# Down pass of a two-layer block on one Trainium2 core: every second weight tile's high half on VectorE, y's rows on SyncE's queue, weight sums ahead of the decode steps

## What is computed

```python
w = NF4_CODE[q.reshape(-1)]                       # 16 codes, q is int32
w = w.reshape(-1, BLOCK) * absmax[:, None]        # one scale for 64 values
g = jnp.einsum('bsh,mh->bsm', x, Wg)              # 2048 tokens, 1024 -> 3584
u = jnp.einsum('bsh,mh->bsm', x, Wu)
h = jax.nn.silu(g) * u
return jnp.einsum('bsm,hm->bsh', h, Wd)           # 3584 -> 1024
x = x + ffn(layernorm(x))                         # the last line of the block
```

## Time and profile before

| | us |
|---|---|
| median of 3 runs | 2045.4 (2044.11 to 2045.6) |
| the profiled execution's own time | 2050.94 |
| its span | 2049.1 |
| TensorE busy | 1948.0 (95%) |
| VectorE busy | 1632.8 (80%) |
| ScalarE busy | 1542.9 (75%) |
| TensorE's granted clock, mean | 0.982 of full speed |

### The profile page before, as it was taken

The page is one execution under the profiler, slowest core; times in us unless marked ns, Lnnn a source line. Parts: engine busy times, 40 slices in busy tenths (PEclk is TensorE's granted clock), DMA queues, the critical chain, the costliest instruction groups (busy, mean ns, idle before and its releaser), DMA issues.

```text
span 2049.1 us, 29927 instructions
## 1 busy us (share of the span) xinstructions
PE 1948.0 (95%) x9872; PEld 987.3 (48%) x9872; DVE 1632.8 (80%) x2716; ACT 1542.9 (75%) x2856; POOL 450.4 (22%) x688
## 2 busy tenths in 40 slices
PE   8989999989999999999999999999999895889999
PEld 3468778744444444444444444444444342334444
DVE  6757789876988898898889889888877677975764
ACT  3768778747989988988998998897999798921100
POOL 0012544540111111121111112112222232222221
PEclk9999999999999999999999999999999997999999
DMA  9012679573644655555564645556677796755443
GB/s 338 25 42 78 186 223 219 168 280 78 154 124 116 138 136 128 124 142 127 120 150 116 136 124 135 128 124 146 166 199 192 192 227 184 177 172 175 165 147 141
DMA packets 387850, 314.63 MB, mean 154 GB/s; under 512 B 327280, under 2 KB 327280, under 8 KB 385776
## 3 DMA queue, kind: packets, MB, share of 16 engines
q1 hardware_dynamic: 334544, 136.00, 30.9%
q0 software_dynamic: 51072, 176.72, 26.3%
q10 hardware_dynamic: 2080, 0.01, 0.1%
HBM read 154.31 MB, written 82.31 MB: 115 GB/s over the span
## 4 chain that ended last, share of the span: by engine, by line
PE 36%; ACT 24%; DVE 21%; issue 10%; DMA 2%; POOL 0%; DVEq 0%; ACTq 0%; SPq 0%; POOLq 0%
PE ps L1978 17%; PE ps L1936 15%; ACT sq L240 8%; ACT sq L236 6%; DVE w L249 4%; DVE tail L2103 2%; ACT halves L287 2%; ACT tail L2009 2%; DVE halves L294 2%; PE ps L1341 1%; ACT tail L2024 1%; PE ps L1302 1%; DMA T<-halves 1%; DVE tail L2069 1%; PE ps L1377 1%
## 5 line engine op out<-in xcount | busy, mean ns | idle before, releaser
L1936 PE MATMUL ps<-T,wS 128*128 128x512 f16 x4704 | 1020.0, 379 | 10.5 <-ACT ps L1993 6.3
L1936 PEld LDWEIGHTS ps<-T,wS 128*128 128x128 f16 x4704 | 458.6, 98 | 568.4 <-issue 15.0
L240 ACT ACTIVATE sq<-sq 128x512 f32<-128x512 f32 x1008 | 572.2, 623 | 0.0
L249 DVE SCALAR_TENSOR_TENSOR w<-sq,w 128x512 f32<-128x512 f32 x672 | 468.5, 697 | 121.2 <-ACT sq L240 108.2
L236 ACT ACTIVATE sq<-q 128x512 f32<-128x512 int32 x672 | 409.4, 628 | 79.8 <-DVE w L249 78.7
L1978 PE MATMUL ps<-T,tail 128*128 128x512 f16 x1584 | 353.3, 385 | 38.9 <-DVE T L2130 34.1
L1978 PEld LDWEIGHTS ps<-T,tail 128*128 128x128 f16 x1584 | 156.4, 99 | 233.4 <-DVE T L2130 36.0
L287 ACT CAST halves<-w 128x512 f16<-128x512 f32 x252 | 154.7, 614 | 52.1 <-DVE w L249 41.0
L1978 PE MATMUL ps<-T,wS 128*128 128x512 f16 x768 | 174.1, 388 | 12.7 <-DVE tail L2150 9.1
L1860 POOL DMA_DIRECT2D keep_h<-tail x196 | 106.3, 542 | 339.6 <-DVE tail L2103 335.1
L2034 ACT CAST T<-w 128x512 f16<-128x512 f32 x56 | 34.5, 617 | 192.6 <-DVE w L2124 192.5
(11 more groups left out here) (216 smaller groups left out, 1861.3 us busy)
## 6 DMA issues: line engine op xcount, KB each, us to landing
keep_h<-tail POOLq DMA_DIRECT2D x196, 256.0 KB, 2.9
tail<-keep_h POOLq DMA_DIRECT2D x66, 512.0 KB, 4.4
wS<-keep_h POOLq DMA_DIRECT2D x32, 512.0 KB, 4.2
q<-in_L_ffn_down_q POOLq DMA_DIRECT2D x56, 256.0 KB, 3.9
q<-in_L_ffn_up_q POOLq DMA_DIRECT2D x52, 256.0 KB, 2.9
q<-in_L_ffn_gate_q POOLq DMA_DIRECT2D x48, 256.0 KB, 3.2
keep_x<-T SPq DMA_DIRECT2D x38, 256.0 KB, 2.8
T<-in_x SPq DMA_DIRECT2D x9, 1024.0 KB, 5.4
```

The source lines that it names most:

```text
L240: nc.scalar.activation(place, place, ACT.Square, bias=b, scale=a).then_inc(un.s_act, 1)
L249: nc.vector.scalar_tensor_tensor(out=un.w[:, buf, :], in0=un.sq[:, (i - 1) % SQ_RING, :], scalar=FACTORS[i - 1][1], in1=un.w[:, buf, :], o ...
L1936: last = nc.tensor.matmul(ps[:, bank, :], un.wS[:, z % SLOTS, a, kt, :], t.Tp[side][product][:, :, b, kt, :], start=fresh and n == 0, stop ...
```

## The change

It has four parts. Every second piece of the down matrix (odd numbers) gets its high half from a VectorE copy between factors 1 and 2 of the next unit, with a semaphore of its own. The quota of VectorE in groups 0 to 2 is 6 instructions in every step. The loads and stores of y's rows go from GpSimd's queue to SyncE's, between the transposes: the stores of a group at the start of the next, the loads at its third step. In VectorE's list of a step the sums stand ahead of the decode instructions; ScalarE's list keeps its order.

```diff
--- before.py
+++ after.py
@@ -130,6 +130,16 @@
     return 2 * pair + (quad in (1, 2)), 2, quad // 2, v % 4
 
 
+def high_on_dve(z):
+
+    return z >= GATE_UP_PIECES and (z - GATE_UP_PIECES) % 2 == 1
+
+
+def highs_on(dve, z):
+
+    return sum(high_on_dve(n) == dve for n in range(z + 1))
+
+
 def last_piece_in(buf, before):
 
     for z in range(before - 1, -1, -1):
@@ -178,6 +188,7 @@
         self.s_add = sem("s_add")
         self.s_turned = [sem(f"s_turned{i}") for i in range(HALF_RING)]
         self.s_whi = sem("s_whi")
+        self.s_dhi = sem("s_dhi")
         self.s_wlo = sem("s_wlo")
 
 
@@ -287,10 +298,21 @@
     nc.scalar.copy(un.halves[:, z % HALF_RING, 0, :], un.w[:, buf, :]).then_inc(un.s_whi, 1)
 
 
+def piece_hi_dve(nc, dve, un, z):
+
+    v = z - GATE_UP_PIECES
+    dve.wait_ge(un.s_fac, STEPS * (GATE_UP_UNITS + v + 1))
+    dve.wait_ge(un.s_turned[z % HALF_RING], 16 * (z // HALF_RING))
+    nc.vector.tensor_copy(un.halves[:, z % HALF_RING, 0, :], un.w[:, v % 4, :]).then_inc(un.s_dhi, 1)
+
+
 def piece_lo(nc, dve, un, z):
 
     buf = PIECE_BUF[z % PIECES] if z < GATE_UP_PIECES else (z - GATE_UP_PIECES) % 4
-    dve.wait_ge(un.s_whi, z + 1)
+    if high_on_dve(z):
+        dve.wait_ge(un.s_dhi, highs_on(True, z))
+    else:
+        dve.wait_ge(un.s_whi, highs_on(False, z))
     nc.vector.scalar_tensor_tensor(out=un.halves[:, z % HALF_RING, 1, :], in0=un.w[:, buf, :], scalar=1.0,
                                    in1=un.halves[:, z % HALF_RING, 0, :], op0=ALU.mult, op1=ALU.subtract).then_inc(un.s_wlo, 1)
 
@@ -327,8 +349,12 @@
     for v in range(DOWN_UNITS):
         for i in range(STEPS):
             yield factor(nc, dve, un, t, GATE_UP_UNITS + v, i)
+            if i == 1 and v > 0 and high_on_dve(GATE_UP_PIECES + v - 1):
+                yield piece_hi_dve(nc, dve, un, GATE_UP_PIECES + v - 1)
             if i == 2 and v > 0:
                 yield piece_lo(nc, dve, un, GATE_UP_PIECES + v - 1)
+    if high_on_dve(GATE_UP_PIECES + DOWN_UNITS - 1):
+        yield piece_hi_dve(nc, dve, un, GATE_UP_PIECES + DOWN_UNITS - 1)
     yield piece_lo(nc, dve, un, GATE_UP_PIECES + DOWN_UNITS - 1)
 
 
@@ -355,9 +381,10 @@
     for v in range(DOWN_UNITS):
         for i in range(OPS):
             yield square(nc, act, un, GATE_UP_UNITS + v, i)
-            if i == 4 and v > 0:
+            if i == 4 and v > 0 and not high_on_dve(GATE_UP_PIECES + v - 1):
                 yield piece_hi(nc, act, un, GATE_UP_PIECES + v - 1)
-    yield piece_hi(nc, act, un, GATE_UP_PIECES + DOWN_UNITS - 1)
+    if not high_on_dve(GATE_UP_PIECES + DOWN_UNITS - 1):
+        yield piece_hi(nc, act, un, GATE_UP_PIECES + DOWN_UNITS - 1)
 
 
 class Plan:
@@ -367,11 +394,13 @@
         fac, add, lo, sq, hi = {}, {}, {}, {}, {}
         d = a = 0
 
-        def dve_unit(u, late):
+        def dve_unit(u, late, copied=None):
             nonlocal d
             for i in range(STEPS):
                 d += 1
                 fac[u, i] = d
+                if i == 1 and copied is not None and high_on_dve(copied):
+                    d += 1
                 for z in late.get(i, ()):
                     d += 1
                     lo[z] = d
@@ -405,17 +434,22 @@
             lo[z], hi[z] = d, a
         for v in range(DOWN_UNITS):
             z = GATE_UP_PIECES + v - 1
-            dve_unit(GATE_UP_UNITS + v, {2: (z,)} if v else {})
-            act_unit(GATE_UP_UNITS + v, {4: (z,)} if v else {})
-        d, a, z = d + 1, a + 1, GATE_UP_PIECES + DOWN_UNITS - 1
-        lo[z], hi[z] = d, a
+            dve_unit(GATE_UP_UNITS + v, {2: (z,)} if v else {}, z if v else None)
+            act_unit(GATE_UP_UNITS + v, {4: (z,)} if v and not high_on_dve(z) else {})
+        z = GATE_UP_PIECES + DOWN_UNITS - 1
+        d += 2 if high_on_dve(z) else 1
+        lo[z] = d
+        if not high_on_dve(z):
+            a += 1
+            hi[z] = a
 
         self.of_act, self.of_dve = {}, {}
         for (u, i), n in fac.items():
             if i > 0:
                 self.of_act[n] = sq[u, READY[i - 1] - 1]
         for z, n in lo.items():
-            self.of_act[n] = hi[z]
+            if z in hi:
+                self.of_act[n] = hi[z]
         for (u, i), n in sq.items():
             f, level = SQUARES[i]
             if level == 0 and u > 0:
@@ -477,7 +511,7 @@
             if k < LATE_SLOTS:
                 return (0, 0, 0, 0, 2, 2, 2, 1, 1, 1, 1)[k], (0, 0, 3, 3, 0, 3, 3, 4, 4, 4, 4)[k]
             return (2 if k // SPLIT_STEPS % 2 or k % 2 else 3), 6
-        return ((5, 6, 5)[(phase - DOWN_PHASE) % 3], 10) if phase - DOWN_PHASE < 3 * CH_PAIRS else (9, 16)
+        return (6, 10) if phase - DOWN_PHASE < 3 * CH_PAIRS else (9, 16)
 
     def sum_steps(self):
 
@@ -1767,8 +1801,8 @@
     s_st = [sem(f"s_st{i}") for i in range(2)]
     s_xy, s_p5, s_z, s_v, s_silu, s_h, s_hsum, s_hhi, s_hlo, s_hd, s_dn, s_yev = (
         sem(n) for n in ("s_xy", "s_p5", "s_z", "s_v", "s_silu", "s_h", "s_hsum", "s_hhi", "s_hlo", "s_hd", "s_dn", "s_yev"))
-    s_wdif, s_wsum, s_wsumhi, s_wsumlo, s_pre, s_fin = (
-        sem(n) for n in ("s_wdif", "s_wsum", "s_wsumhi", "s_wsumlo", "s_pre", "s_fin"))
+    s_wdif, s_wsum, s_wsumhi, s_wsumlo, s_pre = (
+        sem(n) for n in ("s_wdif", "s_wsum", "s_wsumhi", "s_wsumlo", "s_pre"))
 
     def product_at(k):
 
@@ -1832,6 +1866,17 @@
         def turns_due(phase):
             for z in PLAN.turns.get(phase, ()):
                 turn_piece(nc, sp, un, t, z)
+
+        def load_y(group, j):
+            tile, cols = out_place(group, j)
+            if group > 1:
+                sp.wait_ge(s_st[(group - 1) % 2], 16 * BANKS * (group // 2))
+            sp.dma_start(t.y_out_rows[j], t.ys[:, tile, cols]).then_inc(s_yl[group % 2], 16)
+
+        def store_y(group, j):
+            tile, cols = out_place(group, j)
+            sp.wait_ge(s_yev, BANKS * group + j + 1)
+            sp.dma_start((t.ys if group in KEPT_GROUPS else t.out_t)[:, tile, cols], t.y_out_rows[j]).then_inc(s_st[group % 2], 16)
 
         for k in range(SLOT_COUNT):
             turns_due(HIDDEN_PHASE + k)
@@ -1839,13 +1884,23 @@
                 if u < PLAN.early_loads:
                     load_unit(nc, sp, un, t, u)
         for m in range(DOWN_STEPS):
+            group, c = m // CH_PAIRS, m % CH_PAIRS
             turns_due(DOWN_PHASE + m)
-        group = PRODUCTS - 1
+            if group > 1 and c == 0:
+                for j in range(BANKS):
+                    store_y(group - 1, j)
+            if group > 0 and c == 2:
+                if group == 1:
+                    sp.wait_ge(s_v, 2 * STAGES)
+                    sp.wait_ge(t.s_store, 16 * BATCH)
+                    for i in range(HST_RING):
+                        sp.wait_ge(s_hst[i], 16 * (FORMS // HST_RING))
+                for j in range(BANKS):
+                    load_y(group, j)
         for j in range(BANKS):
-            tile, cols = out_place(group, j)
-            sp.wait_ge(s_yev, BANKS * group + j + 1)
-            sp.dma_start(t.out_t[:, tile, cols], t.y_out_rows[j]).then_inc(s_fin, 16)
-        sp.wait_ge(s_fin, 16 * BANKS)
+            store_y(PRODUCTS - 1, j)
+        for i in range(2):
+            sp.wait_ge(s_st[i], 16 * BANKS * 3)
 
     def gpsimd(pool):
         def loads_due(phase):
@@ -1870,17 +1925,6 @@
                     pool.wait_ge(s_hst[n % HST_RING], ring_count(n, HST_RING))
                 nc.gpsimd.dma_start(t.h_in[m % H_RING].rearrange("p n a d -> p n (a d)"), t.hs[form, pair]).then_inc(s_hl[m % H_RING], 16)
 
-        def load_y(group, j):
-            tile, cols = out_place(group, j)
-            if group > 1:
-                pool.wait_ge(s_st[(group - 1) % 2], 16 * BANKS * (group // 2))
-            nc.gpsimd.dma_start(t.y_out_rows[j], t.ys[:, tile, cols]).then_inc(s_yl[group % 2], 16)
-
-        def store_y(group, j):
-            tile, cols = out_place(group, j)
-            pool.wait_ge(s_yev, BANKS * group + j + 1)
-            nc.gpsimd.dma_start((t.ys if group in KEPT_GROUPS else t.out_t)[:, tile, cols], t.y_out_rows[j]).then_inc(s_st[group % 2], 16)
-
         for k in range(SLOT_COUNT):
             stores_due(k)
             loads_due(HIDDEN_PHASE + k)
@@ -1890,25 +1934,11 @@
         for m in range(EARLY_H, H_RING):
             load_h(m)
         for m in range(DOWN_STEPS):
-            group, c = m // CH_PAIRS, m % CH_PAIRS
             for ahead in range(Q_AHEAD + 1) if m == 0 else (Q_AHEAD,):
                 if m + ahead < CH_PAIRS:
                     stores_due(SLOT_COUNT + m + ahead)
                 loads_due(DOWN_PHASE + m + ahead)
             load_h(m + H_RING)
-            if 1 <= c <= 4 and group > 1:
-                store_y(group - 1, 2 * c - 2)
-                store_y(group - 1, 2 * c - 1)
-            if 6 <= c <= 9 and group > 0:
-                if m == CH_PAIRS + 6:
-                    pool.wait_ge(s_v, 2 * STAGES)
-                    pool.wait_ge(t.s_store, 16 * BATCH)
```

(8 more changed lines are left out.)

## The result

| | before | changed | changed, measured again |
|---|---|---|---|
| median, us (executions) | 2044.88 (7) | 2062.47 (7) | 2054.5 (6) |
| lowest to highest | 2043.12 to 2051.61 | 2053.16 to 2072.09 | 2049.03 to 2056.48 |
| ratio to before, 95% | | 1.0078 [1.005, 1.0106] | 1.0040 [1.0011, 1.0069] |
| profiled execution / its span | 2050.94 / 2049.1 | 2055.0 / 2053.2 | 2054.09 / 2052.3 |

**Slower**, by 0.4 to 0.8%. The forecast was no change (2047.4), its range ended at 2060. The first median lies outside, the second inside. The 2044.88 is of seven executions of the kernel before, three of which gave the 2045.4 that the forecast started from.

What follows compares the result with a forecast made beforehand. Only the start of step 51, released by VectorE's sum 9, sets the time: -0.5 + 2.5 for transposes, 2 us later than the profiled 2050.94, which is 5.5 above the median, gives 2047.4 us; range 2032 to 2060.

Steps and rivals of the forecast that it cites:

- The copies: VectorE's copies for odd pieces: 0.48 us each, bounds 0.41 to 0.68; each removes 0.52 us from ScalarE.
- Group 0: First group of the down pass: ScalarE has six copies fewer, TensorE starts step 14 at 1546.2, 2.7 us gained.
- Groups 1 and 2 on VectorE: Wait for y's rows gone in group 1; group 2's banks emptied at 1697.4, 17.5 us earlier.
- t0: Moment VectorE has emptied group 2's banks, before group 3's sums: 1714.97 before, forecast at 1697.4.
- The sums ahead: Group 3: ScalarE idles while VectorE sums, then VectorE waits for ScalarE's list; 102 us instead of 85.0.
- y's rows on SyncE's queue: Eight 256 KB transfers go in front of transposes: 0 to 7.2 us, 2.5 taken, for group 2's loads.
- 60 us of lead: Group 1: y's rows requested two steps into the group, some 60 us ahead, so their wait is gone.
- transposes stand behind y's rows: Rival, chance 0.2: late transposes at pieces 32 and 46 cost 3 + 10 us more; 2060.
- y's rows still come late in group 1: Rival, chance 0.08: SyncE's queue hangs or GpSimd's loads of h starve; t0 8 us later, 2055.
- The baseline: Forecast taken against the profiled execution, 2050.94, which lies 5.5 us above the median of 2045.4.

Runs made afterwards that it cites:

- changed_paced: The changed kernel with y's loads one a step (steps 3 to 10 of a group) instead of eight at once; 2045.26 us, ratio 0.9995.
- hi_first: The changed kernel with ScalarE's copies for the sums also moved ahead of its squares; 2047.13 us, ratio 1.0016.
- sums_back: The changed kernel with the sums behind the decode instructions of their step again; 2035.01 us, ratio 0.9946.
- y_back: The changed kernel with y's loads and stores on GpSimd's queue as before; 2068.79 us, ratio 1.0122.
- sums_only: The kernel before with only the sums moved ahead of the decode instructions on VectorE; 2063.82 us, ratio 1.0108.
- hi_first_h_first: hi_first with loads of h ahead of the codes' on GpSimd's queue from group 1 on; 2043.41 us, ratio 0.9987.
- sums_back_h_first: sums_back with loads of h ahead of the codes' on GpSimd's queue from group 1 on; 2038.77 us, ratio 0.9970.
- sums_back_paced: sums_back with y's loads one a step (steps 3 to 10 of a group) instead of eight in step 3; 2023.75 us, again 2025.82.

## Why the prediction was wrong in size

- **The copies: right.** The row at 1703.88 has 0.42 us, near the lower bound of 0.41 (0.48 was taken, five copies, 0.3 us; scaled from 447 ns by the length alone it would have been 0.51). The Trainium skill's VectorE: DVE Perf Modes (Mode 2×_2P) had spoken for the lower end, and the row agrees. Group 0: TensorE starts step 14 76.2 us after the start, 75.2 predicted.
- **Groups 1 and 2 on VectorE: right, if transfers don't disturb them.** With the loads spread, t0 comes after 226.9 to 227.2 us in four profiles of three kernels (228.5 in a fourth kernel), 226.4 predicted.
- **The sums ahead: right, within 0.3 us.** 101.7 added up and 102 taken; 102.0 measured twice, 102.1 in changed_paced. The waits of 2.3 to 4.3 us for ScalarE were predicted at 2 to 4, and TensorE waits before steps 43, 46, 47, 50 and 51, as named. hi_first shows the cause: ScalarE's unmoved list. One small term has no row: of the 0.26 us of an exchange, 0.12 were put down to a full length, where the rows leave 0.08 (0.69 less 0.61); over eight that is 0.3 us.
- **y's rows on SyncE's queue: this step failed**, "I take 2.5, near the lower end". Its price was 9.2 to 9.5 us at t0 (236.4 less 227.2 or 226.9), above even the upper end of 7.2, and in sums_back's profile, with the same instructions up to t0, 16.1 (243.3 less 227.2). The term counted only TensorE's own waits for transposes in group 2. What came first was a load of h at step 18, which stood on another queue and took 12.4 us beside the burst: 6.05 us of waiting and 2.5 more at the lower clock. By the end of group 1 TensorE was 5.54 us behind VectorE, and 2.42 more in group 2. Together with 1.0 in group 0 and 1.2 that group 1 took longer on VectorE, less 0.1 in group 2, that is the 10.0 us from 226.4 to 236.4. The 1.2 is the burst's too, as far as the rows tell: ScalarE waited 1.23 us for a held-up load of codes, and in changed_paced both are gone. The "60 us of lead" in the sum said when they must land, and nothing of whom they hold up when they all start at once. changed_paced takes this term out and gives 2045.26; the prediction without its 2.5 says 2044.9. That the two are so close is partly luck, for its down pass is 575.9 us and the prediction without the 2.5 has 574.0.
- **The rival "transposes stand behind y's rows" (0.2)** had a price (2060) between the two medians and part of the mechanism. Its 3 us at step 32 came (3.15, for a transpose of 11.6 us); its 10 us at piece 46 are in neither profile. The transposes right behind the burst took 15.5 and 12.2 us, and with the loads spread at most 5.9 us in group 1 and 9.9 in group 2 (7.4 and 12.5 in the kernels that also load h first). This also agrees with the Trainium skill's DMA: Bandwidth & Descriptors (Queues, rings and completion order), which says that an engine takes one ring's descriptors in order: I had named it and set it aside for a median of 3.1 that was taken on a queue without such loads, and in group 3 alone. The same trace has medians of 3.7 and 5.2 us in groups 1 and 2, where the transposes were to stand behind the loads. The rows can't tell that order from the load on the DMA engines as such, since loads on the other queue were held up too. But the waits for late transposes that y_back (7.7 us), sums_only (8.66) and hi_first (14.1) show come near the end of the decode, on kernels with and without y's rows on that queue. Their condition is a sum right behind the low half on VectorE, which is the sums' part of the change.
- **The rival "y's rows still come late in group 1" (0.08)** came nearest in its second condition, that GpSimd's loads of h starve beside the loads of y. It named t0 8 us later and 2055; t0 is 10.0 later and the two profiled executions have 2055.0 and 2054.09. But y's rows were in time, and the loss went by TensorE's wait for h and not by VectorE's wait for y's rows.
- **The baseline.** The sum went against the profiled execution and then down by its 5.5 us to the median. That fits, since the changed kernel's down pass begins 5.5 us sooner (1465.53 against 1471.03), but it is not shown: the start wanders by 14.5 us in one kernel, and no execution of the kernel before at its median was profiled. The +9.5 of the down pass on 2045.4 makes 2054.9, like the profiled 2055.0 and 2054.09 and the second median of 2054.5. The first median, 2062.47, lies 7.6 us above that, and it is this part that carries it out of the range.

**What stays open.** The first measurement's executions reach 2072. Its profile fell on the second fastest of seven, and the second measurement's on one at its median; both have transposes of 6.3 to 7.2 us near 1780. Two things could make the slower ones, and no profile of the changed kernel tells them apart. Late transposes near the end of the decode, waited for in full, are what y_back, hi_first and sums_only suggest; two of these have no burst of y's loads on SyncE's queue and still spread over 18 and 22 us. A dearer burst before t0 is what sums_back's profile suggests, 6.9 us later at t0 than the changed kernel's with the same instructions. Spreading the loads makes t0 steady (226.9 to 227.2 in four profiles), but changed_paced still ranges from 2039.99 to 2052.43. Why transposes near the end of the decode take 14 to 18 us in some executions is not settled either: loads of h stand close together beside them, but of the four profiles with those loads first two still have it, and profiles without that edit have it or not.

## What to carry to other kernels

Work moved ahead on one in-order engine needs its partner on the other engine moved with it; add up, per round, what each engine does while the other waits, since that sum was right here within 0.3 us of 102. Where the moved work reads what a DMA has to bring, count the instructions between the request and the reader: nine of them had hidden a transfer of 14 us. And loads with a lead of 60 us were harmless here only when they were spread: eight at once held up both the transposes on their own queue and the loads of h and of codes on another one, and cost 9 to 16 us by the profile.

## What the runs showed that I had not expected

- A transpose of one weight tile lands after 3.0 to 3.1 us at the shortest. In the changed kernel's profile the first two behind eight loads of 256 KB took 15.5 and 12.2 us in group 1 and 11.6 and 8.7 in group 2; near the end of the decode of hi_first one took 18.5 us beside six loads of 512 KB on the other queue.
- The loads on GpSimd's queue are hit by the same burst. TensorE waited for h at step 18 for 6.85 us in sums_back, 8.28 in hi_first, 6.05 and 4.29 in the changed kernel, 8.36 in hi_first_h_first and 1.86 in sums_back_h_first, and 0.25 us or less at steps 17 and 18 in changed_paced and both runs of sums_back_paced. The kernel before has one wait for h in the whole down pass, 0.7 us. ScalarE's waits for codes in groups 1 and 2 are 1.2 to 12.8 us in the first six profiles and none in the last three.
- The start of the down pass moved by 14.5 us between two profiles of one kernel (sums_back_paced). A stage measured from its own start agreed to 0.1 us between executions where no late transfer was waited for (group 3 of the changed kernel: 102.0 and 102.0); where transfers were late it did not (to t0 with the burst, same instructions: 236.3 to 243.3).
